# Heads stage: stacked q and k in six wide transfers, last batch's output rows by halves of heads

## The reference

```python
q = (x @ Wq.T + bq).reshape(B, T, 16, 16).transpose(0, 2, 1, 3)   # k, v alike; the second block has no bias
logits = jnp.einsum('bhqd,bhkd->bhqk', q, k) / jnp.sqrt(D)
attn = softmax(where(causal, -inf, logits))
out = jnp.einsum('bhqk,bhkd->bhqd', attn, v).transpose(0, 2, 1, 3).reshape(B, T, C)
y = out @ Wo.T + bo
```

## Time and profile before

| what | us |
|---|---|
| median of 3 runs | 2983.54 |
| lowest, highest | 2978.67, 2984.82 |
| profiled execution, its own time | 2974.38 |
| its span, first to last instruction | 2972.6 |
| first heads stage, about | 745 to 1290 |
| second heads stage, about | 2175 to 2725 |
| TensorE busy over the span | 2472.1 (83%) |

### The profile page before, as it was taken

One profiled execution on the slowest core, in us unless ns is written; L12 is line 12 of the kernel. 1 busy time (PEld: TensorE's weight loads), 2 busy tenths in 40 slices (PEclk: granted clock), 3 DMA queues, 4 the chain that ended last, 5 costly groups with the idle time before them and its releaser, 6 DMA issues. The chain is left out here.

```text
span 2972.6 us, 49393 instructions
## 1 busy us (share of the span) xinstructions
PE 2472.1 (83%) x15186; PEld 1598.4 (54%) x15186; DVE 1951.5 (66%) x5464; ACT 1459.7 (49%) x3374; POOL 1131.3 (38%) x1578
## 2 busy tenths in 40 slices
PE   7965995788699889859929984996869999984998
PEld 6755994455133323348719973774623333333776
DVE  6854885576688768458728864773658877843444
ACT  3433552333277768624405542433627877772433
POOL 4774444665232222217754436650122222220000
PEclk9987997899699999979969996998969999997999
DMA  4453554454665666144435544331574656524000
GB/s 133 171 145 128 178 180 152 152 180 147 79 104 96 83 103 108 61 143 148 170 104 176 179 151 138 112 96 54 162 111 83 98 91 117 90 59 156 29 29 29
DMA packets 266560, 351.35 MB, mean 118 GB/s; under 512 B 41873, under 2 KB 196034, under 8 KB 266306
## 3 DMA queue, kind: packets, MB, share of 16 engines
q1 hardware_dynamic: 226370, 239.08, 35.2%
q0 software_dynamic: 39936, 109.11, 10.8%
HBM read 197.32 MB, written 149.95 MB: 117 GB/s over the span
## 5 line engine op out<-in xcount | busy, mean ns | idle before, releaser
L1180 DVE CUSTOM_DVE_ANT_0 attn_heads_masked_s<-attn_heads_s_ps,attn_heads_causal 128x768 bf16<-128x768 f32 (+7 forms) x1024 | 727.6, 754 | 214.5 <-PE attn_heads_s_ps L1008 212.8
L1118 ACT ACTIVATE attn_heads_probs<-attn_heads_st_ps 128x512 f32<-128x512 f32 (+3 forms) x1536 | 662.9, 494 | 270.2 <-PE attn_heads_st_ps L1027 256.9
L1008 PE MATMUL attn_heads_s_ps<-attn_heads_k_st,attn_heads_q_st 96*128 96x512 bf16 (+3 forms) x1536 | 410.3, 348 | 92.4 <-DMA attn_heads_k_st<-k_dram 77.7
L1027 PE MATMUL attn_heads_st_ps<-attn_heads_q_st,attn_heads_k_st 99*128 99x512 bf16 (+3 forms) x1536 | 427.2, 337 | 4.3 <-ACT attn_heads_probs L1118 3.6
L1043 PE MATMUL attn_heads_o_ps<-attn_heads_probs,attn_v_sb 128*32 128x512 f32 (+3 forms) x3072 | 335.0, 509 | 2.9 <-POOL attn_heads_probs L958 2.3
L1027 PEld LDWEIGHTS attn_heads_st_ps<-attn_heads_q_st,attn_heads_k_st 99*128 99x128 bf16 x1536 | 136.9, 98 | 350.7 <-ACT attn_heads_probs L1118 251.8
L958 POOL TENSOR_SCALAR_AFFINE_SELECT attn_heads_probs<-attn_heads_probs 128x512 f32<-128x512 f32 x256 | 163.7, 640 | 404.8 <-ACT attn_heads_probs L1118 399.7
L1463 POOL DMA_INDIRECT xs_dram<-moe_route_xn,rows_at x256 | 272.6, 1065 | 79.0 <-issue 76.4
L1008 PEld LDWEIGHTS attn_heads_s_ps<-attn_heads_k_st,attn_heads_q_st 96*128 96x128 bf16 x1536 | 137.2, 101 | 218.5 <-DMA attn_heads_k_st<-k_dram 83.0
L1958 POOL DMA_DIRECT2D ys_dram<-moe_expert_y_sb x288 | 158.0, 549 | 243.6 <-DVE moe_expert_y_sb L2076 243.6
L2032 ACT ACTIVATE moe_expert_xT_hi<-moe_expert_xT_ps 128x256 fp32r<-128x256 f32 x288 | 110.9, 385 | 196.2 <-PE moe_expert_xT_ps L1976 195.9
(11 more groups left out here) (263 smaller groups left out, 5941.8 us busy)
## 6 DMA issues: line engine op xcount, KB each, us to landing
moe_expert_x_sb<-xs_dram SPq DMA_DIRECT2D x288, 128.0 KB, 2.1
ys_dram<-moe_expert_y_sb POOLq DMA_DIRECT2D x288, 128.0 KB, 2.1
attn_heads_q_st<-q_dram SPq DMA_DIRECT2D x192, 128.0 KB, 8.7
attn_heads_k_st<-k_dram SPq DMA_DIRECT2D x192, 128.0 KB, 9.1
o_dram<-attn_heads_oT SPq DMA_DIRECT2D x64, 256.0 KB, 5.8
moe_route_w_raw<-in_L_ffn_we_dram SPq DMA_DIRECT2D x96, 128.0 KB
q_dram<-attn_proj_parts SPq DMA_DIRECT2D x32, 384.0 KB, 2.9
k_dram<-attn_proj_parts SPq DMA_DIRECT2D x32, 384.0 KB, 3.1
```

What stands on the lines that cost most here:

```text
L1008: last = pe.matmul(s_ps[:, at + a // TILE, 0:w], q_st[0:DEPTH, r, h, i * P:(i + 1) * P], k_st[0:DEPTH, r, h, a:a + w], start=True, stop=True)
L1027: pe.matmul(st_ps[:, v % NB, 0:w], k_st[0:ROWS, n % R, h, j * P:(j + 1) * P], q_st[0:ROWS, n % R, h, first:first + w], start=True, stop=Tr ...
L1118: act.activation(probs[:, G % NR, h, 0:w], st_ps[:, v % NB, 0:w], ACT.Exp, scale=scale)\
L1180: dve.tensor_tensor_reduce(out=masked_s[:, use % 4, 0:w], in0=s_banks[:, at * TILE:at * TILE + w], in1=causal[:, SEQ - w:SEQ], scale=1.0, ...
```

## The change

**Layout in DRAM.** The columns of the q and k weights are written in another order when they are rounded (`in_order`, `by_dim`), so within each half of the heads the rows of q and k in DRAM go by dimension first and then by head. Four heads of a quad then lie side by side, and a row of the stack is one piece of 8 KB. The bias is loaded by four small DMAs instead of two.

**Loads.** `load(n)` issues six DMAs: for q and k each one of 48 partitions, one of 32 and one of 16. The source of the first q DMA is indexed by part (3), dimension (16), and 4096 values. For k the part's index has step zero: one part is read three times.

**Output rows.** All rows, sums, inverses and rounded or split values are handled by halves of heads, `kd` = 0 and 1. For the last batch the first half is loaded behind loop 14 and inverted and spread in loop 15. The second half of the last tile has its inverses issued by ScalarE's queue.

The core of the diff:

```diff
-    LOAD = 12 * 16
+    LOAD = 2 * SPLIT * 16
...
-                    rows = slice(quad * QUAD * HD, (quad + 1) * QUAD * HD)
-                    q_v = [q_dram[b, l, rows, :].rearrange("(h d) t -> d h t", d=HD) for l in range(SPLIT)]
-                    k_v = [k_dram[b, l, rows, :].rearrange("(h d) t -> d h t", d=HD) for l in range(SPLIT)]
-                    for at, (ql, kl) in enumerate(((0, 0), (1, 0), (2, 0), (0, 1), (1, 1), (0, 2))):
-                        to = slice(at * HD, (at + 1) * HD)
-                        sp.dma_start(q_st[to, r, :, :], q_v[ql]).then_inc(stack_loaded[r], 16)
-                        sp.dma_start(k_st[to, r, :, :], k_v[kl]).then_inc(stack_loaded[r], 16)
+                    rows = slice(quad // 2 * P, (quad // 2 + 1) * P)
+                    q_v, k_v = (x[b, :, rows, :].rearrange("l (d q h) t -> l d q (h t)", d=HD, h=QUAD)[:, :, quad % 2, :] for x in (q_dram, k_dram))
+                    for l in range(SPLIT):
+                        at, count = sum(SPLIT - m for m in range(l)), SPLIT - l
+                        to = slice(at * HD, (at + count) * HD)
+                        sp.dma_start(q_st[to, r, :, :], q_v[0:count]).then_inc(stack_loaded[r], 16)
+                        sp.dma_start(k_st[to, r, :, :], k_v[l:l + 1].to_broadcast([count, HD, QUAD * SEQ])).then_inc(stack_loaded[r], 16)
...
+                    if n == NQ - 2:
+                        load_rows(EARLY, 0)
+                        load_rows(EARLY + 1, 0)
...
+                    if n == NQ - 1:
+                        for t in (EARLY, EARLY + 1):
+                            put_inverses(sp, t, 0)
+                        for t in (EARLY, EARLY + 1):
+                            spread_inverses(sp, t, 0)
...
-                round_rows(len(ROUND_AFTER))
-                copy_out(NQ - 1, 1)
-                for t in range(len(ROUND_AFTER) + 1, TILES):
-                    round_rows(t)
+                for t in range(len(ROUND_AFTER), TILES - 1):
+                    for kd in range(KD):
+                        round_rows(t, kd)
+                    if t == len(ROUND_AFTER):
+                        copy_out(NQ - 1, 1)
+                    elif t == EARLY - 2:
+                        put_inverses(act, TILES - 1, 1)
+                    elif t == EARLY - 1:
+                        spread_inverses(act, TILES - 1, 1)
+                for kd in range(KD):
+                    round_rows(TILES - 1, kd)
...
-                    act.activation(w_hi[:, n, :, :], w_raw[:, n, :, :], ACT.Copy).then_inc(w_hi_ready, 1)
+                    act.activation(in_order(w_hi, n), by_dim(w_raw, n), ACT.Copy).then_inc(w_hi_ready, 1)
```

More of the change, by code:

```diff
@@ L255, in _ @@
                     for n in range(2):
-                        sp.dma_start(b_col[:, 2 * n:2 * n + 2], b_qkv[n].rearrange("(m p) -> p m", p=P),
-                                     allow_slow_non_contiguous=True).then_inc(b_loaded, 16)
+                        for m in range(KD):
+                            some = b_qkv[n][m * P:(m + 1) * P].rearrange("(h d) -> d h", d=HD)
+                            sp.dma_start(b_col[:, 2 * n + m:2 * n + m + 1], some, allow_slow_non_contiguous=True).then_inc(b_loaded, 16)
                     sp.dma_start(bv_row[:, :], b_qkv[2].rearrange("(a d) -> a d", a=1)).then_inc(b_loaded, 16)
@@ L709, in heads_phase @@
     HALVES = SEQ // TILE
-    SUMS = P // HEADS
+    SUMS = P * KD // HEADS
     EARLY = TILES - HALVES
+    LATE = [(EARLY, 0), (EARLY + 1, 0), (EARLY, 1), (EARLY + 1, 1)]
     def unit_over(g):
@@ L1189, in _ @@
                     if b > 0 and quad == 2 and k in INVERT_AFTER:
-                        invert((b - 1) * HALVES + INVERT_AFTER.index(k))
+                        for kd in range(KD):
+                            invert((b - 1) * HALVES + INVERT_AFTER.index(k), kd)
                 copy_turn(NQ - 1)
+                invert(EARLY, 0)
+                invert(EARLY + 1, 0)
                 for t in range(TILES):
-                    split(t)
-                    if t > 0:
+                    if t == TILES - 1:
+                        split(t, 0)
                         add_output(t - 1)
-                    if t == 1:
-                        invert(EARLY)
-                    elif t == 3:
-                        normalise(EARLY)
-                        invert(EARLY + 1)
-                    elif t == 5:
-                        normalise(EARLY + 1)
+                        normalise(t, 1)
+                        split(t, 1)
+                    else:
+                        for kd in range(KD):
+                            split(t, kd)
+                        if t == EARLY - 2:
+                            invert(EARLY + 1, 1)
+                        if t > 0:
+                            add_output(t - 1)
+                    if t == 1:
+                        invert(EARLY, 1)
+                    elif t == 2:
+                        normalise(EARLY, 0)
+                        normalise(EARLY + 1, 0)
+                    elif t == 4:
+                        normalise(EARLY, 1)
                 add_output(TILES - 1)
```

146 lines of the change are left out of this document (75 added, 71 removed).

## The result

| | us |
|---|---|
| kernel before, median of 4 runs | 2982.18 (2978.67 to 2984.82) |
| changed kernel, median of 4 runs | 3310.95 (3303.22 to 3320.01) |
| ratio | 1.1104, 95% interval 1.1073 to 1.1135 |
| profiled execution, span | 3308.4 (before 2972.6) |
| predicted | 3231, range 3110 to 3370 |

The change costs 329 us where 247 were forecast. The direction and the mechanism are as predicted. One term was too small, the time that a stack takes to land.

What follows compares the result with a forecast made beforehand. Stages run one behind the other, bound in the heads stages by TensorE's waits for stacks. 2974.4 + 213 (loops) + 49 (start) - 15 (end) + 0.5 (weights) = 3222 us profiled, 3231 against the median; range 3110 to 3370.

Steps and rivals of the forecast that it cites:

- Engines: Stack loads: the outermost source dimension caps engines at 3, 2 and 16, with q and k on the same ones.
- A: Rival for stack loads: all sixteen engines work, a stack lands in 8.5 us, 93 us saved, 2890 us; chance 0.07.
- B: Rival for stack loads: few engines, but landing within 18.3 us; only the end gains, about 2970 us; chance 0.03.
- Rival C: Stack loads: few engines at 17.7 GB/s each, a load takes 30.5 us, +250 us, 3480 us; chance 0.06.
- A load lands 24.3 us after its issue: Stack loads: 1.6 us to start, then 22.7 us for 540.7 thousand bytes on the busiest engine at 23.8 GB/s.
- A plain loop 35.1 us: Heads-stage loop without other transfers: 24.3 us landing, 8.4 us remainder, 2.4 us slow clock; 26.7 us before.
- A loop with other transfers 41 us: Five of 13 loops with a load, where rows, x or inverses go ahead of it: 41 us on average.
- Loops in sum: Loops with a load, both heads stages: 486 us each against 384 and 375, costing 213 us.
- The start +24.5 us a stage: Start of each heads stage: the first maxima's put waits behind three loads, delaying loop 0; +49 us in all.
- The end -7.5 us a stage: Last tile of each heads stage: earlier inverses save 7.5 of 8.45 us waiting, -15 us in all.
- Weights +0.5: Strided rounding of q and k weights: 0 at equal speed, 2.4 us at half speed; 0.5 us taken.
- The range: Whole kernel, 3110 to 3370: 62 us less without slow clock, 70 less at 10% better rate, 150 more toward Rival C.

Runs made afterwards that it cites:

- the half dose: The changed kernel with only the three q DMAs indexed by dimension first, the k DMAs left on 3, 2 and 16 engines: ratio 1.0293 to the kernel before.
- the run with the blocks turned round: The changed kernel with the stacks' blocks in the order 16, 32, 48 rows, so 48-partition DMAs write partitions 48 to 95: ratio 1.0899 to the kernel before.
- the repeat: The changed kernel run again without any edit, on another chip: ratio 1.1109 to the kernel before.

## Why the prediction was right, and which term was mis-sized

**Engines: right.** The prediction took 3, 2 and 16 engines from the shares of three other transfers. The trace shows 3.0 and 2.1. That q and k use the same engines, which no row had shown, holds too: with other engines for k, the two-engine stretch would show four. Rivals A and B fall with this, and the run with the dimension outermost shows what A would have brought: 2%, some 60 us, where A had priced 93. Rival C, 17.7 GB/s an engine, was too slow for the changed kernel (21.3 on average, below), though the half dose shows about that rate (17.4).

**A load lands 24.3 us after its issue: too short.** This is the term that was mis-sized. The score tile that needs the stack runs on average 27.9 us after the issue in the eight plain loops of the first stage and 27.3 in the second. By the packets in the trace, averaged over the sixteen, these 27.6 us are 1.5 to the first packet (forecast 1.6), 25.3 for the packets of the load (forecast 22.7), and 0.7 from the end of the last packet to TensorE's start, a term that the forecast had left out. So the 540.7 thousand bytes of the busiest engine moved at 21.3 GB/s instead of 23.8. I had carried the rate of eight engines over to two and three, though the width and place of what they write differ. An undisturbed engine is faster, 26 GB/s, and would have moved them in 20.8 us. Two things bring this to 25.3. About 2 us are the collision of three engines in partitions 0 to 47, as the run with the blocks turned round shows. The other 2.4 us are still there in that run. By the packets most of them fall in the opening of a load, where its last two DMAs and an output run on all engines (894 to 899: share 0.52 at 134 GB/s, 16 GB/s an engine); the half dose shows the same slowing. How they divide among the loads' own narrow DMAs and the outputs was not tried. That 23.8 came this near is partly luck: the engines were faster than assumed, and this hid 1.9 of some 5 us that the forecast did not have.

**A plain loop 35.1 us: 38.3.** The 10.8 us behind the stack hold to the tenth, the slow clock (0.77) among them. The measured loops, 38.7 and 37.9 us in the two stages, are 3.2 us longer than forecast for the reason above. Over 16 plain loops that is 51 us. (Before the change a loop took 26.7.)

**A loop with other transfers 41 us: 43.7.** The five loops average 44.2 and 43.2 us. Over ten loops that is 27 us more. The longer landing alone would account for it: from a plain loop to one of these it is 5.4 us, where I had put down 5.9. No run takes these loops apart.

**Loops in sum:** +147.9 and +145.1 us, forecast 102 and 111. The two terms above are 78 of these 80 us, and the 80 are the whole miss.

**The start +24.5 us a stage: +26.2 and +26.9.** Three loads went out first, and the put, issued at 805.22, let TensorE go on at 821.75, 16.5 us later, behind the third load. The run with the put moved ahead shows that this was the cause. The forecast had loop 0 at 819, and it began at 821.75. (819 is 24.1 us after the 794.85 of before, not 24.5.) One thing wasn't seen: with the put out of the way the loss would mostly return one loop later.

**The end -7.5 us a stage: -3.0 and -9.3**, from loop 15 to the last output product (64.5 and 67.2 before, 61.5 and 57.9 after). In the repeat it is 57.2 and 56.9, so the -3.0 is on the low side. The three pairs of kernels with and without the halves give 13 to 22 us for both stages; 15 was forecast.

**Weights +0.5: at most about 1.** Per attention step two rounding instructions take 0.43 us more each on ScalarE, and two subtractions some 0.32 on VectorE. The stages account for 334.7 of the 335.8 us by which the spans differ; the other 1.1 us have room for part of this and little else.

**The range.** Its ends don't follow from the terms named beside it. The two reductions, 62 and 70 us, lead to 3099 and not 3110; half of C's 250 us is 125 and leads to 3356, while 150 would give 3381. The measured 3311 lies inside either way.

In sum: loops +293, start and the loop behind it +54, end -12, rest +1, makes 336 for the profiled executions.

## What to carry to other kernels

Before making DMAs fewer and wider, look at what stands outermost in their source and destination. The changed kernel and the fastest one differ in the order of two dimensions and in nothing else, and are 13% apart. The DMA share of a stretch tells how many engines work (share times 16), and it tells it in advance, from other transfers of the same kernel. Once the count is known, the bytes on the busiest engine give the landing, but the rate depends on what else runs and where it writes: take it as a range (17 to 26 GB/s here), not from the one row that looks nearest.

## What the runs showed of the hardware

- One engine moves 26 GB/s in 8 KB pieces: 55 GB/s in the stretch with two at work, and 78 for three that write partitions 48 to 95. Three that write partitions 0 to 47 move 63.
- Sixteen engines that write 16 partitions at a time move 118 to 131 GB/s, and the pieces' size (8 or 2 KB) makes no gain. Writing 48, 32 and 16 partitions at a time they move 160 to 178.
- SyncE's issue of a DMA took 0.4 to 0.8 us as a rule, but mostly 4.3 to 5.6 us (753.67 to 772.72) at the start of the stage, from the second load on, while the engines were still busy with the first. The same six DMAs on sixteen engines were issued in 0.4 to 0.6 us each at that place, and before the change an issue took 0.43 us. The put was issued some 8 us after the last of these loads, so no cost can be seen here, but transfers that queue up on few engines can hold up the engine that issues them.
